# Second feed-forward layer of the last four groups as three products of high and low parts

## The chip, the cores and the metric

The kernel runs on one core of a Trainium2 chip. The core has TensorE (PE in the profile, its weight loads PEld), VectorE (DVE), ScalarE (ACT), GpSimd (POOL) and SyncE (SP), which run side by side and wait for each other through semaphores. The metric is the device time of one execution in microseconds (us); lower is better.

## The reference, cut to what matters

A graph layer is followed by a gated feed-forward layer. The change touches only the second matrix product of the feed-forward layer, `h @ w2`:

```python
x = x + gnn(layernorm(x), adj, ...)
h2 = layernorm(x)
weights = h2 @ wr + br                       # one weight for each node
sel_idx = top_k(weights, k)[:kk]             # 511 of 1024 nodes, for each of 8 batches
h = gelu(sel @ w1 + b1)                      # 128 -> 512
y = (h @ w2 + b2) * w_sel                    # 512 -> 128
x = x + h2 + scatter(y at sel_idx)
```

All values are 32-bit floats.

## The kernel before, in words

`build` writes one program for each engine by hand, so the order of the work on an engine is the order of its code, and semaphores (names in `_ok`, `_ps`, `_in`) carry results from one engine to another. First come eight batches of the graph layer. Then comes the feed-forward stage, in `NG = 9` groups b = 0..8 of 512 columns each: seven groups hold the chosen rows of batches 0 to 6, the last two hold all 1024 rows of batch 7. Buffers alternate with p = b % 2.

One group passes these steps:

- `sel_to_features(b)` (TensorE, L1577): four transposes bring the rows into bank D0. `hi_of_sel` (ScalarE, L881) rounds them to the fp32r format (high part, `xTH`), and `lo_of_sel` (VectorE, L1250) writes the rest (low part, `xTL`).
- `up(b, p, j)`, j = 0..3 (TensorE, L1590): the first layer. Each is done by `three` (L1353): high weight times high input, high times low, low times high, three fp32r matmuls of 512 columns into one of the banks C0, C1, D1 in turn.
- `gelu(b, p, j)` (ScalarE, L885) turns the bank into `g[p][j]`, plain fp32, in SBUF, and frees the bank.
- `down(b, p, j)` (TensorE, L1600): the second layer, one plain fp32 matmul of 512 columns with `wf2[:, j]` for each j, summed in bank N0 or N1. The profile records it as two halves.
- `update(b, p)` (ScalarE, L893) adds the bias, `update_back` (TensorE, L1613) transposes back into M0 (one buffer), `updated_rows(b, p)` (VectorE, L1274) scales and adds the base rows, and `rows_home` (GpSimd, L583) scatters each 128 rows into the output with an indirect DMA. For the last two groups `last_rows` (L1264) and a plain DMA take its place.

TensorE's order in a group is up(b,3), down(b,0), up(b+1,0), down(b,1), update_back(b-1), up(b+1,1), down(b,2), up(b+1,2), down(b,3), sel_to_features(b+2). The wait that matters later: up(b+1,0) needs `lo_of_sel(b+1)`, whose rows were transposed at the end of the group before. VectorE also ranks the weights of the last batch in groups 2 to 4 (`rank`) and ends that with `kept_weights` (L1254, three small instructions).

`wc2` holds the convolution weights, 128 partitions x 2 x (N_TAP x 128) fp32r. No matmul reads it after the last batch's convolution.

Of the kernel before, what the change touches and what calls it, by code (L numbers as in the profile page):

```python
# [19 lines left out]
ALU = mybir.AluOpType  # L20
ACT = mybir.ActivationFunctionType

P = 128
B = 8
N = 1024
T = N // P
D = 128
HALF = 512
# [13 lines left out]
HT = HID // D  # L42
# [15 lines left out]
UV_FOR = {0: 2, 1: 3, NU // 2: 4}  # L58
N2_AT = (5, 6, 7, 8)
EARLY = {3: 0, 7: 1, 11: 2}  # L60


C_ID, C_TRI, C_MASK = 0, P, 2 * P
# [31 lines left out]
V_BIH, V_BHH, V_F1, V_F2, V_BR, V_BSE, V_MSG = 8, 11, 14, 18, 19, 20, 21  # L95
# [51 lines left out]
def build(nc, x, adj, vectors, weights, conv2_w, const, out):  # L147
    ctx = ExitStack()
    with ctx:
        def sb(name, shape, dt=F32):  # L150
            return ctx.enter_context(nc.sbuf_tensor(name, shape, dt))
# [4 lines left out]
        def sem(name):  # L156
            return ctx.enter_context(nc.semaphore(name))

        def f32(ap):
            return ap.bitcast(F32)  # L160
# [10 lines left out]
        def col(k, n=1):  # L171
            return vec[:, k:k + n]
# [9 lines left out]
        wc2 = sb("wc2", [P, 2, N_TAP * D], F32R)  # L182

        def weight(at):
# [27 lines left out]
        wf2 = msgF[:, 0:HT, :]  # L212
# [14 lines left out]
        g = [[xflat[:, j * HALF:(j + 1) * HALF] for j in range(HT)],  # L227
             [xflat[:, (HT + j) * HALF:(HT + j + 1) * HALF] for j in range(2)] + [xT[:, 0, half_] for half_ in
                                                                                  (slice(0, HALF), slice(HALF, N))]]
# [31 lines left out]
        Db, Mb, Nb, Cb = (D0, D1), (M0, M1), (N0, N1), (C0, C1)  # L261
# [24 lines left out]
        c2_ps, xcH_ok, xcL_ok = sem("c2_ps"), sem("xcH_ok"), sem("xcL_ok")  # L286
# [18 lines left out]
        f1_ps, g_ok, f2_in = sem("f1_ps"), sem("g_ok"), sem("f2_in")  # L305
# [2 lines left out]
        y_ps, y_ok, yb_ps, O_ok = sem("y_ps"), sem("y_ok"), sem("yb_ps"), sem("O_ok")  # L308
        out_done = [sem("out_done0"), sem("out_done1")]
        place_ok, kept_ok, last_out = sem("place_ok"), sem("kept_ok"), sem("last_out")  # L310

        up_banks = (C0, C1, D1)
        LU = len(up_banks)

        def wait(eng, s, b, per, k):

            v = b * per + k
            if not isinstance(v, int) or v > 0:
                eng.wait_ge(s, v)
# [23 lines left out]
        def half(h):  # L343
            return slice(h * HALF, (h + 1) * HALF)
# [322 lines left out]
        def _(act):  # L667
# [70 lines left out]
            def row_of_weights(b, h, bank_):  # L738

                wait(act, wt_ps, b, NH, h + 1)  # L740
                wait(act, rank_ok, b - 1, T, T)
                nc.scalar.activation(W[:, half(h)], bank_[:, :], ACT.Copy).then_inc(W_ok, 1)  # L742
# [142 lines left out]
            def gelu(b, p, j):  # L885

                wait(act, f1_ps, b, HT, j + 1)
                if j == 0:
                    wait(act, y_ps, b - 2, 1, 1)
                nc.scalar.activation(g[p][j], up_banks[(HT * b + j) % LU][:, :], ACT.Gelu_apprx_tanh,  # L890
                                     bias=col(V_F1 + j)).then_inc(g_ok, 1)

            def update(b, p):  # L893
                wait(act, y_ps, b, 1, 1)
                wait(act, yb_ps, b - 2, 1, 1)
                nc.scalar.activation(Y[:, p, :], Nb[p][:, :], ACT.Identity, bias=col(V_F2)).then_inc(y_ok, 1)

            def ffn_step(b, q, first, last):
                if first:
                    hi_of_sel(0, 0)  # L900
                gelu(b, q, 0)
                if first:
                    candidate(B - 1, 1)
                    hi_of_sel(1, 1)
                gelu(b, q, 1)
                gelu(b, q, 2)
                if not first and not last:
                    hi_of_sel(b + 1, 1 - q)
                if b == 2:
                    row_of_weights(B - 1, 0, M1)  # L910
                if not first:
                    update(b - 1, 1 - q)
                gelu(b, q, 3)
                if b == 2:
                    row_of_weights(B - 1, 1, M1)

            over_groups(ffn_step)
            update(NG - 1, (NG - 1) % 2)
# [3 lines left out]
        def _(dve):  # L922
            TS, TT, STT = nc.vector.tensor_scalar, nc.vector.tensor_tensor, nc.vector.scalar_tensor_tensor
# [185 lines left out]
            def node_weights(b, q):  # L1109

                wait(dve, prod_ok, b, NH, NH)
                nc.vector.tensor_reduce(wv[:, :].rearrange("p (k t) -> p k t", k=NH), prod, mybir.AxisListType.X,
                                        ALU.add).then_inc(dot_ok, 1)
                wait(dve, dot_ok, b, 1, 1)
                TS(R[:, q, :, R_W], wv[:, :], col(V_BR), None, ALU.add).then_inc(w_ok, 1)
# [20 lines left out]
            def rank(b, q, t):  # L1136
                rank_tiles_ahead(b, q, t)
                rank_tiles_behind(b, q, t)
# [111 lines left out]
            def lo_of_sel(b, p):  # L1250
                wait(dve, xsH_ok, b, 1, 1)
                TT(xTL[:, 0, half(p)], D0[:, :], f32(xTH[:, 0, half(p)]), ALU.subtract).then_inc(xsL_ok, 1)

            def kept_weights():  # L1254

                b = B - 1
                dve.wait_ge(rank_ok, T * B)
                TT(acc[:, 1, :], acc[:, 1, :], acc[:, 2, :], ALU.add).then_inc(sum_ok, 1)
                dve.wait_ge(sum_ok, NH * b + 1)
                TT(rankF[:, :], acc[:, 0, :], acc[:, 1, :], ALU.add).then_inc(place_ok, 1)  # L1260
                dve.wait_ge(place_ok, 1)
                STT(kept[:, :], rankF[:, :], float(KEEP), R[:, 1, :, R_W], ALU.is_lt, ALU.mult).then_inc(kept_ok, 1)
# [11 lines left out]
            def updated_rows(b, p):  # L1274

                if b >= NXS:
                    last_rows(b, b - NXS)
                    return
                wait(dve, yb_ps, b, 1, 1)
                if b > 1:  # L1280
                    dve.wait_ge(out_done[p], 16 * TH * (b // 2))
                for c in range(TH):
                    xs = Xs[:, b, c, :]
                    STT(O[:, p, c, :], M0[:, c * P:(c + 1) * P], xs[:, R_W:R_W + 1], xs[:, D:2 * D], ALU.mult,  # L1284
                        ALU.add).then_inc(O_ok, 1)
# [27 lines left out]
            def ffn_step(b, q, first, last):  # L1313
                if first:
                    new_gate(B - 1, 1)
                    lo_of_sel(0, 0)
                    rank(B - 2, 0, 6)
                    rank(B - 2, 0, 7)
                    indices(B - 2, 0, 1)
                    blend(B - 1, 1)  # L1320
                    lo_of_sel(1, 1)
                    state_to_nodes(B - 1, (M1, N1))
                    moments2(B - 1)
                    mean_and_variance(1, stats2, T * B)
                elif not last:
                    lo_of_sel(b + 1, 1 - q)
                if b == 1:
                    last_norm()
                    last_products()
                    node_weights(B - 1, 1)  # L1330
                if b in (2, 3, 4):
                    rank(B - 1, 1, 3 * (b - 2))
                if not first:
                    updated_rows(b - 1, 1 - q)
                if b == 1:
                    last_base(0)
                    last_base(1)
                if b in (2, 3, 4):
                    rank(B - 1, 1, 3 * (b - 2) + 1)
                if b in (2, 3):  # L1340
                    rank(B - 1, 1, 3 * (b - 2) + 2)
                if b == 4:
                    kept_weights()

            over_groups(ffn_step)
# [4 lines left out]
        def _(pe):  # L1350
            MM, TR = nc.tensor.matmul, nc.tensor.transpose

            def three(out_, wgt, hi, lo, start, stop):  # L1353

                MM(out_, wgt(0), hi, start=start, stop=False)  # L1355
                MM(out_, wgt(0), lo, start=False, stop=False)  # L1356
                return MM(out_, wgt(1), hi, start=False, stop=stop)  # L1357
# [68 lines left out]
            def conv_odd(b):  # L1426
# [4 lines left out]
                for out_, at, row in ((N1[:, 0:Q], T_WOC, 0), (C0[:, 0:Q], T_WO, 1), (C0[:, Q:2 * Q], T_WO + KQ, 2)):  # L1431
# [4 lines left out]
                    for k in range(KQ):  # L1436
                        if n in EARLY:
                            front(b, EARLY[n])
                        n += 1
# [160 lines left out]
            def down(b, p, j):  # L1600
                wait(pe, g_ok, b, HT, j + 1)
                if j == 0:
                    if b == 0:
                        pe.wait_ge(f2_in, 16)
                        pe.wait_ge(q2_ok, NH * B)
                    if b == 1:
                        pe.wait_ge(x1_ok, NH * B)
                    wait(pe, y_ok, b - 2, 1, 1)
                i = MM(Nb[p][:, :], wf2[:, j, :], g[p][j], start=j == 0, stop=j == HT - 1)  # L1609
                if j == HT - 1:  # L1610
                    i.then_inc(y_ps, 1)

# [60 lines left out]
```

## Time and profile before

| | us |
|---|---|
| median of 3 runs | 564.97 (563.96 to 565.4) |
| the profiled execution, device time | 564.87 |
| its span, first to last instruction | 562.3 |
| TensorE busy | 545.6 (97%) |
| VectorE busy | 475.0 (84%) |
| ScalarE busy | 354.9 (63%) |
| GpSimd busy | 275.7 (49%) |

The device time lies 2.6 us above the span. Busy shares are means over the whole program, and matmuls are recorded longer than the step from one to the next, so the order of events in the stage decides, not the share. In the chain of waits (the work that ended last, followed back) each piece is the time that a step really added. Of the 40 slices of the page, the feed-forward stage is the last five or so (from about 488 us on); there TensorE shows 9 tenths throughout, while VectorE falls from 9 to 2 tenths after 530 us. The granted TensorE clock is 1.00 from 494 us to 555 us.

### The profile page before, as it was taken

How to read it: one execution, taken by the hardware profiler on the slowest of the kernel's cores; microseconds unless marked ns; L12 is line 12 of the kernel's file. 1: busy time of each engine (PE TensorE's matmuls, PEld its weight loads, DVE VectorE, ACT ScalarE, POOL GpSimd, SP SyncE). 2: the span in 40 equal slices, each digit the busy share in tenths (PEclk: the TensorE clock that was granted, in tenths of full speed). 3: DMA queues.
4: the chain of work that ended last, by engine and by line, in shares of the span. 5: the costliest groups of instructions: out<-in, count | busy, mean ns of one | idle time of the engine just before them, and what ended most of it. 6: DMA issues, size and time to landing. Idle time of an engine off the chain costs nothing.

```text
span 562.3 us, 9026 instructions
## 1 busy us (share of the span) xinstructions
PE 545.6 (97%) x2964; PEld 416.6 (74%) x2964; DVE 475.0 (84%) x1048; ACT 354.9 (63%) x616; POOL 275.7 (49%) x346
## 2 busy tenths in 40 slices
PE   7799999999999999999999999999999999899996
PEld 3786798678966896689767986798678966666663
DVE  6987478679898989899898989899979987978722
ACT  4856475856686577747674857575856673555552
POOL 2740354325358344834484546654545365536552
PEclk9999999999999999999999999999999999899999
DMA  8602700180008300650047001800171006402111
GB/s 274 278 2 76 300 0 2 45 308 23 2 0 270 142 2 1 193 220 1 1 124 289 1 2 52 323 2 1 46 283 46 1 1 191 148 16 81 36 36 61
DMA packets 33339, 54.52 MB, mean 97 GB/s; under 512 B 2098, under 2 KB 23051, under 8 KB 33166
## 3 DMA queue, kind: packets, MB, share of 16 engines
q1 hardware_dynamic: 29710, 48.42, 24.7%
q0 software_dynamic: 3584, 5.54, 2.8%
q8 instruction: 23, 0.38, 0.3%
q14 instruction: 22, 0.18, 0.1%
HBM read 44.21 MB, written 13.43 MB: 103 GB/s over the span
## 4 chain that ended last, share of the span: by engine, by line
PE 86%; DVE 8%; ACT 3%; DMA 2%; issue 1%; SPq 0%; DVEq 0%; ACTq 0%
PE N L1504 20%; PE M L1481 10%; PE C L1355 7%; PE C L1357 7%; PE C L1356 7%; PE D L1475 5%; PE N L1609 5%; PE N L1355 4%; PE N L1356 3%; PE N L1357 3%; ACT hab L674 2%; DVE tr L1014 2%; PE M L1356 2%; PE M L1355 2%; PE M L1357 2%; PE D L1355 2%
## 5 line engine op out<-in xcount | busy, mean ns | idle before, releaser
L780 ACT ACTIVATE tr<-D 128x512 f32<-128x512 f32 x128 | 76.4, 597 | 76.9 <-PE D L1475 75.2
L1481 PEld LDWEIGHTS M<-cst,adjb 128*128 128x128 f32 x512 | 63.9, 141 | 35.2 <-issue 21.2
L1475 PE MATMUL D<-V,U 128*128 128x512 f32 x128 | 89.3, 698 | 0.0
L1481 PE MATMUL M<-cst,adjb 128*128 128x128 f32 x512 | 76.8, 273 | 0.6 <-DVE ga L1101 0.6
L578 POOL DMA_INDIRECT sel<-R,ridx x56 | 61.1, 1090 | 16.0 <-issue 14.0
L1504 PE MATMUL N<-ga,msgF 128*128 128x512 f32 x128 | 64.2, 594 | 0.0
L1504 PE MATMUL N<-tz,msgF 128*128 128x512 f32 x128 | 64.2, 594 | 0.0
L1355 PE MATMUL C<-zR,wc 128*128 128x256 f32 x208 | 60.6, 291 | 0.6 <-DVE zR L1023 0.6
L1356 PE MATMUL C<-zR,wc 128*128 128x256 f32 x208 | 58.7, 282 | 0.0
L1357 PE MATMUL C<-zR,wc 128*128 128x256 f32 x208 | 58.6, 282 | 0.0
L1131 DVE TENSOR_SCALAR_CACHE_REDUCE junk<-W,R 128x1024 bf16<-128x1024 f32 (+3 forms) x64 | 51.7, 808 | 3.9 <-ACT W L742 3.9
L1101 DVE TENSOR_TENSOR ga<-tr,M 128x512 f32<-128x512 f32 x64 | 43.5, 680 | 9.6 <-ACT tr L780 9.4
L1101 DVE TENSOR_TENSOR tz<-tr,M 128x512 f32<-128x512 f32 x64 | 43.7, 684 | 8.5 <-ACT tr L780 6.7
L523 POOL TENSOR_TENSOR ga<-xT,gn 128x512 f32<-128x512 f32 x16 | 22.7, 1421 | 45.2 <-ACT gn L828 44.3
L624 POOL TENSOR_TENSOR wk<-tz,xT 128x512 f32<-128x512 f32 x8 | 12.4, 1556 | 61.2 <-DVE tz L1036 61.2
L1125 DVE TENSOR_SCALAR_CACHE_REDUCE junk<-W,R 128x128 bf16<-128x128 f32 (+6 forms) x56 | 41.4, 739 | 0.0
L1475 PEld LDWEIGHTS D<-V,U 128*128 128x128 f32 x128 | 24.3, 190 | 22.9 <-ACT tr L780 19.1
L605 POOL TENSOR_TENSOR junk<-hab 128x521 f32<-128x521 f32 x16 | 20.1, 1256 | 41.6 <-ACT hab L674 41.6
L1355 PEld LDWEIGHTS C<-zR,wc 128*128 128x128 f32 x208 | 39.3, 189 | 0.8 <-issue 0.8
L1356 PEld LDWEIGHTS C<-zR,wc 128*128 128x128 f32 x208 | 39.4, 189 | 0.0
L1357 PEld LDWEIGHTS C<-zR,wc 128*128 128x128 f32 x208 | 39.4, 189 | 0.0
L589 POOL DMA_INDIRECT out<-xn,adjb x28 | 28.4, 1013 | 20.3 <-DVE xn L1284 13.9
(236 smaller groups left out, 1527.6 us busy)
## 6 DMA issues: line engine op xcount, KB each, us to landing
adjb<-in_adj SPq DMA_DIRECT2D x8, 4096.0 KB, 14.9
adjb<-sel SPq DMA_DIRECT2D x7, 516.0 KB, 5.3
xall<-in_x SPq DMA_DIRECT2D x7, 512.0 KB, 5.2
out<-R SPq DMA_DIRECT2D x7, 512.0 KB, 3.5
R<-in_conv_w SPq DMA_DIRECT2D x1, 1088.0 KB, 8.6
sel<-R,ridx POOLq DMA_INDIRECT x56
xall<-in_weights SPq DMA_DIRECT2D x1, 832.0 KB, 11.0
xall<-in_x SPq DMA_DIRECT2D x2, 256.0 KB, 2.9
```

Of the source, the lines that this page charges most:

```text
L578: nc.gpsimd.indirect_dma_start(sel[b], bass.IndirectOffsetOnAxis(ap=ridx[:, q, t:t + 1], axis=0), R[:, q, t, :], None, bounds_check=KEEP - ...
L589: nc.gpsimd.indirect_dma_start(out_rows, bass.IndirectOffsetOnAxis(ap=at, axis=0), O[:, p, c, :], None, bounds_check=B * N - 1, oob_is_err ...
L780: nc.scalar.activation(E[:, u % NE, :], Db[u % NH][:, :], ACT.Exp, scale=-1.0).then_inc(exp_ok, 1)
L1101: TT(A[u % NA], E[:, u % NE, :], Mb[u % NH][:, :], ALU.mult).then_inc(A_ok, 1)
L1125: TS(junk[:, t % 2, 0:t * P], W[:, 0:t * P], R[:, q, t, R_W:R_W + 1], None, ALU.is_ge, ALU.add, accum_out=acc[:, 0, t:t + 1])
L1131: TS(junk[:, k, t * P:N], W[:, t * P:], w, None, ALU.is_gt, ALU.add, accum_out=acc[:, 1, t:t + 1])
L1355: MM(out_, wgt(0), hi, start=start, stop=False)
L1356: MM(out_, wgt(0), lo, start=False, stop=False)
L1357: return MM(out_, wgt(1), hi, start=False, stop=stop)
L1475: MM(Db[h][:, :], U[:, t * P:(t + 1) * P], V[:, half(h)], start=True, stop=True).then_inc(d_ps, 1)
L1481: i = TR(Mb[h][:, k * P:(k + 1) * P], adjb[:, h * TH + k, t * P:(t + 1) * P], ident)
L1504: MM(Nb[h][:, :], msgF[:, t, :], A[v % NA], start=t == 0, stop=t == T - 1).then_inc(nm_ps, 1)
```

## The change

Groups 5 to 8 (`b >= G3`, `G3 = 5`) compute `down` with `three` as well. That needs high and low parts of the weights and of the activations; both lie in `wc2`. ScalarE writes the high part of `wf2` (`hi_of_f2`, in group 3) and VectorE its low part (`lo_of_f2`, in group 4). Of the activations, ScalarE writes the high part for j = 0 and j = 3, by a second evaluation of the gelu from the same bank ahead of the plain one; VectorE copies it for j = 1 and j = 2 and subtracts for all four (`parts_of_g`). `kept_weights` moves from VectorE's group 4 to group 5.

```diff
+G3 = 5
+        f2S = wc2[:, :, 0:HT * D]
+        def g_parts(p, j):
+            at = HT * D + (HT * p + j) * HALF
+            return wc2[:, :, at:at + HALF]
 # ScalarE, gelu
-                nc.scalar.activation(g[p][j], up_banks[(HT * b + j) % LU][:, :], ACT.Gelu_apprx_tanh,
+                up_ = up_banks[(HT * b + j) % LU]
+                if b >= G3 and j in (0, HT - 1):
+                    nc.scalar.activation(g_parts(p, j)[:, 0], up_[:, :], ACT.Gelu_apprx_tanh, bias=col(V_F1 + j))
+                nc.scalar.activation(g[p][j], up_[:, :], ACT.Gelu_apprx_tanh,
                                      bias=col(V_F1 + j)).then_inc(g_ok, 1)
+            def hi_of_f2():
+                act.wait_ge(f2_in, 16)
+                act.wait_ge(c2_ps, 2 * B)
+                nc.scalar.activation(f2S[:, 0], wf2[:, :, :].rearrange("p j d -> p (j d)"),
+                                     ACT.Copy).then_inc(f2H_ok, 1)
 # ScalarE, end of a group
+                if b == G3 - 2:
+                    hi_of_f2()
 # VectorE
+            def lo_of_f2():
+                dve.wait_ge(f2H_ok, 1)
+                TT(f2S[:, 1], wf2[:, :, :].rearrange("p j d -> p (j d)"), f32(f2S[:, 0]),
+                   ALU.subtract).then_inc(f2L_ok, 1)
+            def parts_of_g(b, p, j):
+                wait(dve, g_ok, b, HT, j + 1)
+                gp = g_parts(p, j)
+                if j not in (0, HT - 1):
+                    nc.vector.tensor_copy(gp[:, 0], g[p][j]).then_inc(gH_ok, 1)
+                    dve.wait_ge(gH_ok, 2 * (b - G3) + j)
+                TT(gp[:, 1], g[p][j], f32(gp[:, 0]), ALU.subtract).then_inc(gL_ok, 1)
 # VectorE, a group, after lo_of_sel(b + 1)
+                if b == G3 - 1:
+                    lo_of_f2()
...
+                if b == G3:
+                    parts_of_g(b, q, 1)
+                    parts_of_g(b, q, 2)
+                if b >= G3:
+                    parts_of_g(b, q, HT - 1)
+                    if not last:
+                        parts_of_g(b + 1, 1 - q, 0)
                 if not first:
                     updated_rows(b - 1, 1 - q)
+                if b >= G3 and not last:
+                    parts_of_g(b + 1, 1 - q, 1)
+                    parts_of_g(b + 1, 1 - q, 2)
+                if b == G3 - 1:
+                    parts_of_g(b + 1, 1 - q, 0)
...
-                if b == 4:
+                if b == G3:
                     kept_weights()
 # TensorE, down
-                i = MM(Nb[p][:, :], wf2[:, j, :], g[p][j], start=j == 0, stop=j == HT - 1)
+                if b < G3:
+                    i = MM(Nb[p][:, :], wf2[:, j, :], g[p][j], start=j == 0, stop=j == HT - 1)
+                else:
+                    if b == G3 and j == 0:
+                        pe.wait_ge(f2L_ok, 1)
+                    wait(pe, gL_ok, b - G3, HT, j + 1)
+                    gp = g_parts(p, j)
+                    i = three(Nb[p][:, :], lambda v: f2S[:, v, j * D:(j + 1) * D], gp[:, 0], gp[:, 1],
+                              j == 0, j == HT - 1)
```

TensorE at the start of group 5, before the change: the transposes of group 6's rows into D, then up(5,3), down(5,0), up(6,0), down(5,1) and the transposes back into M.

```order
L1587 MATMUL D<-cst,adjb 128x128 [waits xsL_ok,sel_in6]
L1587 MATMUL D<-cst,adjb 128x128 x3
L1355 MATMUL D<-xTH,wall 128x512 [waits g_ok,xsL_ok]
L1356 MATMUL D<-xTL,wall 128x512
L1357 MATMUL D<-xTH,wall 128x512
L1609 MATMUL N<-xall,msgF 128x512 [waits y_ok,g_ok]
L1355 MATMUL C<-xTH,wall 128x512 [waits g_ok,xsL_ok]
L1356 MATMUL C<-xTL,wall 128x512
L1357 MATMUL C<-xTH,wall 128x512
L1609 MATMUL N<-xall,msgF 128x512 [waits g_ok]
L1619 MATMUL M<-cst,wk 128x128 [waits y_ok,O_ok]
```

The same place after the change (L1404 to L1406 are `three`).

```order
L1636 MATMUL D<-cst,adjb 128x128 [waits xsL_ok,sel_in6]
L1636 MATMUL D<-cst,adjb 128x128 x3
L1404 MATMUL D<-xTH,wall 128x512 [waits g_ok,xsL_ok]
L1405 MATMUL D<-xTL,wall 128x512
L1406 MATMUL D<-xTH,wall 128x512
L1404 MATMUL N<-wc 128x512 [waits f2L_ok,gL_ok,y_ok,g_ok]
L1405 MATMUL N<-wc 128x512
L1406 MATMUL N<-wc 128x512
L1404 MATMUL C<-xTH,wall 128x512 [waits g_ok,xsL_ok]
L1405 MATMUL C<-xTL,wall 128x512
L1406 MATMUL C<-xTH,wall 128x512
L1404 MATMUL N<-wc 128x512 [waits gL_ok,g_ok]
```

Nothing changes its place on TensorE; each down into N becomes three matmuls from `wc2`, and the first of them waits for `gL_ok` besides.

VectorE from the end of group 4 to group 6, before: `kept_weights` (three rows), `lo_of_sel(6)`, `updated_rows(4)`, `lo_of_sel(7)`.

```order
L1258 TENSOR_TENSOR acc<-acc 128x8 [waits rank_ok]
L1260 TENSOR_TENSOR rankF<-acc 128x8 [waits sum_ok]
L1262 SCALAR_TENSOR_TENSOR kept<-rankF,R 128x8 [waits place_ok]
L1252 TENSOR_TENSOR xTL<-D,xTH 128x512 [waits xsH_ok]
L1284 SCALAR_TENSOR_TENSOR xn<-M,adjb 128x128 [waits out_done0,yb_ps]
L1284 SCALAR_TENSOR_TENSOR xn<-M,adjb 128x128 x3
L1252 TENSOR_TENSOR xTL<-D,xTH 128x512 [waits xsH_ok]
```

After, from `updated_rows(4)` (L1319) to `lo_of_sel(7)` (L1272). Ahead of this piece, between `lo_of_sel(6)` and `updated_rows(4)`, stand CAST and TENSOR_TENSOR for g(5,1), the same for g(5,2), and one TENSOR_TENSOR each for g(5,3) and g(6,0).

```order
L1319 SCALAR_TENSOR_TENSOR xn<-M,adjb 128x128 [waits out_done0,yb_ps]
L1319 SCALAR_TENSOR_TENSOR xn<-M,adjb 128x128 x3
L1285 CAST wc<-xall 128x512 [waits g_ok]
L1287 TENSOR_TENSOR wc<-xall,wc 128x512 [waits gH_ok]
L1285 CAST wc<-xall 128x512 [waits g_ok]
L1287 TENSOR_TENSOR wc<-xall,wc 128x512 [waits gH_ok]
L1293 TENSOR_TENSOR acc<-acc 128x8 [waits rank_ok]
L1295 TENSOR_TENSOR rankF<-acc 128x8 [waits sum_ok]
L1297 SCALAR_TENSOR_TENSOR kept<-rankF,R 128x8 [waits place_ok]
L1272 TENSOR_TENSOR xTL<-D,xTH 128x512 [waits xsH_ok]
```

`lo_of_sel(7)` followed `updated_rows(4)` directly before; now seven instructions stand between them, four of them of 512 columns.

## Rows read from the trace of the kernel before

**Rows 1.** The page, part 1: busy us, share of the span, instructions.

```profile
PE 545.6 (97%) x2964; PEld 416.6 (74%) x2964; DVE 475.0 (84%) x1048; ACT 354.9 (63%) x616; POOL 275.7 (49%) x346
```

**Rows 2.** Windows: stretch, length, busy of each engine, clock, DMA share, GB/s.

```profile
541.00:548.00 7.00, 7.00 (x28) 4.33 (x27) 1.81 (x5) 3.59 (x7) 3.88 (x4) 1.00 0.11 37
```

**Rows 3.** Chain of waits, from 480 us on: start us, us added, engine, tile, line.

```profile
530.53 0.44 PE D L1587 x4
...
533.34 0.86 PE N L1609 x2
...
537.75 0.44 PE D L1587 x4
538.19 0.23 PE C L1355
...
539.75 0.35 PE C L1355
...
540.56 0.86 PE N L1609 x2
...
544.97 0.43 PE D L1587 x4
...
552.88 1.72 PE N L1609 x4
...
555.03 1.73 PE N L1609 x4
```

**Rows 4.** Timeline, ScalarE, 538 us: start us, us, engine, line, operation.

```profile
538.23 0.60 ACT L883 ACTIVATE xTH<-D 128x512 fp32r<-128x512 f32 x1 [0.61 <-PE D L1587]
538.72 0.68 ACT L896 ACTIVATE wk<-N,vec 128x512 f32<-128x512 f32 x1
539.29 0.69 ACT L890 ACTIVATE xall<-C,vec 128x512 f32<-128x512 f32 x1
```

**Rows 5.** Timeline, VectorE, 530 to 539 us.

```profile
530.22 0.17 DVE L1258 TENSOR_TENSOR acc<-acc 128x8 f32<-128x8 f32 x1
...
530.62 0.17 DVE L1262 SCALAR_TENSOR_TENSOR kept<-rankF,R 128x8 f32<-128x8 f32 x1
531.63 0.69 DVE L1252 TENSOR_TENSOR xTL<-D,xTH 128x512 fp32r<-128x512 f32 x1 [0.84 <-ACT xTH L883]
534.68 1.13 DVE L1284 SCALAR_TENSOR_TENSOR xn<-M,adjb 128x128 f32<-128x128 f32 x4 [2.35 <-PE M L1619]
538.86 0.69 DVE L1252 TENSOR_TENSOR xTL<-D,xTH 128x512 fp32r<-128x512 f32 x1 [3.06 <-ACT xTH L883]
```

**Rows 6.** Groups of VectorE by form: busy us, mean ns, idle before.

```profile
L1005 DVE TENSOR_TENSOR xTL<-xT,xTH 128x512 fp32r<-128x512 f32 x16 | 10.4, 684 | 0.5 <-ACT xTH L805 0.5
...
L1131 DVE TENSOR_SCALAR_CACHE_REDUCE junk<-W,R 128x512 bf16<-128x512 f32 x8 | 5.9, 741 | 0.0
...
L998 DVE MEMSET hab<- 128x1044 f32 x1 | 0.9, 928 | 0.2 <-issue 0.2
```

**Rows 7.** Timeline, GpSimd beside VectorE, 401 to 414 us.

```profile
401.83 2.18 POOL L568 TENSOR_TENSOR R<-xall,R 128x1024 f32<-128x1024 f32 x1
...
403.27 0.89 DVE L1132 SCALAR_TENSOR_TENSOR junk<-W,R,cst 128x128 bf16<-128x128 f32 x1
...
406.67 1.09 DVE L1088 SCALAR_TENSOR_TENSOR zR<-wk,zR 128x512 fp32r<-128x512 f32 x1
...
406.86 1.74 POOL L578 DMA_INDIRECT sel<-R,ridx  x1 [0.30 <-issue]
...
412.74 0.97 POOL L578 DMA_INDIRECT sel<-R,ridx  x1 [0.30 <-issue]
...
412.89 0.35 DVE L1132 SCALAR_TENSOR_TENSOR junk<-W,R,cst 128x128 bf16<-128x128 f32 x1
```

**Rows 8.** Timeline, GpSimd, its last scatter.

```profile
554.15 0.97 POOL L589 DMA_INDIRECT out<-xn,adjb  x1 [0.30 <-issue]
```

**Rows 9.** DMA issues: KB each, median us from issue to landing.

```profile
out<-xn,adjb POOLq DMA_INDIRECT x28, 2.3
```

More of the change, by code:

```diff
@@ L310, in build @@
         place_ok, kept_ok, last_out = sem("place_ok"), sem("kept_ok"), sem("last_out")
+        gL_ok, f2H_ok, f2L_ok, gH_ok = sem("gL_ok"), sem("f2H_ok"), sem("f2L_ok"), sem("gH_ok")
+        f2S = wc2[:, :, 0:HT * D]
+        def g_parts(p, j):
+            at = HT * D + (HT * p + j) * HALF
+            return wc2[:, :, at:at + HALF]
         up_banks = (C0, C1, D1)
```

## The prediction

> **What bounds the kernel now.** I read the page's busy shares first: TensorE is busy 545.6 of the 562.3 us [rows 1]. Then the windows over the tail, since the change lives there: in the seven microseconds from 541 us TensorE is busy for all 7.00, ScalarE 3.59, VectorE 1.81, GpSimd 3.88, at a granted clock of 1.00 [rows 2]. So TensorE's stream is the bound in groups 5 to 8, and VectorE and ScalarE have room on average. Third, the chain of waits, because it gives what each step really adds: a plain fp32 down is 0.86 us, each fp32r matmul of `three` 0.23 us, four transposes 0.44 us [rows 3]. From one `sel_to_features` to the next is 544.97 - 537.75 = 7.22 us, a group.
>
> The chain also has a small wait in each group: the first matmul of up(b+1,0) is 0.35 us instead of 0.23 at 539.75 [rows 3]. The timelines say why. The transposes end at 538.19; `hi_of_sel` runs 538.23 to 538.83, `lo_of_sel` 538.86 to 539.55 [rows 4, 5]; the next down starts at 540.56 [rows 3]. Less three matmuls (0.69) the first one begins at 539.87, so a low part that ends at time t lets TensorE begin at t + 0.32. This chain is independent of how long down(b,0) takes. It is the row that limits what the change can give.
>
> **The sum, part by part.** All of it is made against the profiled execution (564.87 us, 2.6 above its span); that lies 0.1 under the median 564.97.
>
> Removed and added on TensorE: 16 downs (groups 5 to 8, j = 0..3). Each goes from 0.86 to 3 x 0.23 = 0.69 or 0.70; I take a saving of 0.165. 16 x 0.165 = 2.65 us, if nothing else waits.
>
> Taken back by `lo_of_sel`: in groups 5, 6, 7 up(b+1,0) already waits 0.12 us for it, so the saving of down(b,0) turns into a longer wait. 3 x 0.165 = 0.5 us. That leaves 2.15 us as the most the order of the code can give.
>
> ScalarE: `hi_of_f2` once (0.62 us or so) falls into group 3, where ScalarE is half idle. The second gelus are two per group. Consecutive ScalarE instructions start 0.57 us apart (538.72 to 539.29 [rows 4]), so ScalarE goes from 3.6 to 4.7 us in a group of about 6.6: hidden. up(b+1,3) needs the bank of gelu(b+1,0), which is free three microseconds earlier. Cost zero.
>
> VectorE: what it did in a group was `lo_of_sel` and `updated_rows`, 1.81 us. Now come four subtractions and two copies. A 512-column subtraction of two SBUF tensors takes 0.684 us [rows 6]; when nothing makes it wait for the one ahead, the next starts 0.60 after its start. An instruction that waits for the one ahead starts 0.03 after its end (530.22 + 0.17 to 530.42 for the three of `kept_weights`, which take 0.57 from start to end [rows 5]).
>
> The copy (CAST, fp32 to fp32r, SBUF to SBUF, one input) is not in the trace. Bounds by the nearest rows: above, a one-input VectorE instruction of 512 columns, 0.741 us; below, the memset of 1044 columns in 0.928 us, half of which is 0.46 [rows 6]. Below that I know no row, and a longer one than 0.74 only if something holds it (below). I take 0.46, since the memset is the other instruction here that only moves data, and keep 0.74.
>
> The Trainium skill, "VectorE: DVE Perf Modes", section on the perf-mode tier table, says that a copy of fp32 within SBUF runs at two elements a cycle and a two-tensor operation at one. Worked out from its formula, an estimate, the copy would take 0.42 us, and the sum would be about 0.2 us better. The trace's 0.684 for the subtraction agrees with one element a cycle; its one-input row at 0.741 (a reduce) does not show the fast form.
>
> Now the order. Group 5 begins as before: transposes of group 6's rows end at 530.97, `lo_of_sel(6)` runs 531.63 to 532.32 [rows 3, 5]. VectorE then copies g(5,1), 532.23 to 532.69, and subtracts to 533.41. down(5,1) can begin at 533.73; before it began at 533.34 [rows 3]. That is 0.39 late, in spite of the saving of down(5,0). The three downs that follow save 0.49, so the transposes of group 7's rows end at about 538.09 (before 538.19).
>
> On VectorE after 533.3: second copy and subtraction (1.09), subtractions for g(5,3) and g(6,0) (1.2), `updated_rows(4)` 535.6 to 536.7 (before 534.68 [rows 5]), then copy, subtraction, copy, subtraction (2.2), then `kept_weights` (0.5). `lo_of_sel(7)` can start at 539.35, where its input is ready at 538.09 + 0.67 = 538.76. It is 0.6 late. It ends at 540.04, up(7,0) runs 540.36 to 541.05, where it had ended at 540.56: now 0.49 behind. Three downs give 0.49 back: at the end of group 6 the change has gained nothing so far.
>
> Group 6: VectorE has no `kept_weights`, but waits for gelu(7,0) (done about 542.35) before it may take `updated_rows(5)` at 543.0; copies and subtractions end so that `lo_of_sel(8)` starts at 546.2, 0.1 late. up(8,0) ends at 547.88 against 547.78. Group 7: three downs, -0.49, net -0.39. Group 8 has no up to wait for: four downs, -0.66, net -1.05. Its tightest wait is g(8,3): up(8,3) ends about 552.5, two gelus and a subtraction end at 554.5, TensorE may start at 554.83 and gets there at 555.03. It just fits.
>
> What stands behind the moved steps: `updated_rows(b-1)` now follows a subtraction that waits for gelu(b+1,0), so it comes 0.4 to 1 us later, and so do the four scatters on GpSimd's queue behind it. The last of these ended at 555.12 and lands 2.3 us after issue [rows 8, 9], before the final rows of a program that ends past 561. Four us of room; cost zero. M0, which `updated_rows` frees, is wanted again five microseconds later.
>
> Sum: 564.87 - 2.65 + 0.5 (the old wait) + 1.1 (VectorE late: 0.39 for down(5,1), 0.6 for `lo_of_sel(7)`, 0.1 for `lo_of_sel(8)`) = 563.82. Against the median, 563.9.
>
> **The rivals.**
>
> A. VectorE is in time. If the copies or the small steps are shorter than I take them, or GpSimd and VectorE overlap better, only the 0.5 us is lost: 564.97 - 2.15 = 562.8. For it: VectorE's 1.81 us in 7 [rows 2]. Against it: the queue ahead of `lo_of_sel(7)` is 7 us of work in a window of 6.4, whatever the copy takes down to about 0.3.
>
> B. Slower: GpSimd holds the copies. VectorE and GpSimd get in each other's way in this trace: a two-input VectorE instruction of 128 columns took 0.89 us while a GpSimd tensor operation ran, against 0.35 elsewhere; an indirect DMA that began inside a two-input VectorE instruction took 1.74 us against 0.97 [rows 7]. But the same two-input instruction ran in its 0.35 beside an indirect DMA in flight (412.74 and 412.89 [rows 7]). What a fast copy does beside one, no row shows. Six copies stand ahead of something that TensorE waits for (four between `lo_of_sel(6)` and `lo_of_sel(7)`, two more ahead of `lo_of_sel(8)`), and the scatters of `rows_home` run for 5.1 of each 7 us. If each copy is held 0.5 us on average, half an indirect DMA, 6 x 0.5 = 3.0: 563.9 + 3.0 = 566.9. It decides from 0.2 us a copy (6 x 0.175 = 1.05 eats the gain); fully held, 0.97 each, it would be 569.7.
>
> The Trainium skill, "SBUF — State Buffer", section on the two separate sides, says just this: a fast-form copy and a GpSimd operation share a port pair under an exclusive lock, the first keeps it for its whole length, and descriptors of indirect DMAs are held up. By that rule the copies make GpSimd late, which costs nothing here, and may be held themselves. The row of 1.74 us agrees with the first half; no row here shows the second.
>
> C. The copy has no fast form and takes as long as the subtraction or the one-input row, 0.69 to 0.74. Six copies, 0.23 to 0.28 longer each: +1.4 to +1.7, so 565.3 to 565.6, no change that can be seen. For it: the slow one-input row. Against it: the memset.
>
> **Chances.** A change under 0.3%, 1.7 us, can't be told from none here; the three runs of before spread over 1.4 us. Forecast 0.50, A 0.15, B 0.15, C 0.20. Faster by over 1.7 us: nearly all of A and a quarter of the forecast, 0.27. Slower by over 1.7 us: most of B, 0.13. The rest, 0.60, is within. The forecast's own range is 563.2 to 564.6. The given range must take in A (562.8) and C (565.6) and part of B: 562.4 to 566.2.
>
> **What would show it.** Right: in the chain of waits the downs of groups 5 to 8 as three pieces of 0.23; groups 5 and 6, from one `sel_to_features` to the next, near 7.1 and 7.3 us and not near 6.7; TensorE waiting for VectorE (`gL_ok`) at down(5,1) and for `lo_of_sel` at up(7,0) by about 0.8 us; the CAST near 0.46 us. A shows as no such wait at up(7,0); B as CASTs of widely different lengths, or as VectorE idle ahead of them while GpSimd runs, and C as a CAST of 0.69. I am wrong altogether if a matmul from `wc2` takes more than 0.23, if down(8,3) waits long for g(8,3), or if the time moves outside this tail.

## The result, and the profile after

The changed kernel takes 565.78 us (median of 16 runs, 565.21 to 566.59) against 564.58 (16 runs, 563.96 to 565.88): a ratio of 1.0021, 95% interval 1.0015 to 1.0028, so 1.2 us slower. I had forecast 563.9, 1.1 us faster than the 564.97 of three runs then known, in the range 562.4 to 566.2. The time is inside the range and on the wrong side.

The profiled execution took 566.05 us with a span of 563.9, 1.6 longer than the span before. The page, part 1, as [rows 1], and the windows view, as [rows 2]:

```profile
PE 543.9 (96%) x2980; PEld 419.3 (74%) x2980; DVE 489.3 (87%) x1073; ACT 360.1 (64%) x625; POOL 277.3 (49%) x346
```

```profile
541.00:548.00 7.00, 6.81 (x33) 5.32 (x33) 5.16 (x11) 4.59 (x9) 3.84 (x5) 1.00 0.11 36
```

TensorE has lost 1.7 us of work and is no longer busy throughout; VectorE went from 1.81 to 5.16 us in these seven. The chain of waits (start us, us added, what) follows the path that the prediction drew, as [rows 3] did:

```profile
530.90 0.45 PE D L1636 x4
531.35 0.02 issue
531.38 0.61 ACT xTH L891
531.99 0.02 issue
532.01 0.69 DVE xTL L1272
532.70 0.53 DVE wc L1285
...
547.05 0.61 DVE xTL L1272
547.66 0.04 issue
547.70 0.50 PE D L1404
...
555.77 0.24 PE N L1404
556.01 0.23 PE N L1405
556.24 0.25 PE N L1406
```

From 532 to 547 it lies mostly on VectorE (between 540.8 and 543.7, left out here, on TensorE and ScalarE), and the downs are three pieces of 0.23 to 0.25, as forecast. Now the ends. The last down ended at 555.03 + 1.73 = 556.76 [rows 3]; it ends at 556.49 here, although this execution was 0.37 late on entering the stretch (530.90 against 530.53). So TensorE gained 0.64 us from there on. VectorE's last rows, in its timeline:

```profile
558.01 1.13 DVE L1307 SCALAR_TENSOR_TENSOR R<-M,kept,R 128x128 f32<-128x128 f32 x4 [1.68 <-PE M L1676]
```

They end at 559.14 (559.41 before). Every row that the chain shows is earlier at the end, and yet the span is 1.6 longer. What is later is on GpSimd, which the chain does not touch. The timeline of VectorE from 547 us (compare the `updated_rows` at 549.12 in the kernel before, not in the rows above) and that of GpSimd, as [rows 8]:

```profile
548.52 0.69 DVE L1287 TENSOR_TENSOR wc<-xT,wc 128x512 fp32r<-128x512 f32 x1 [0.87 <-ACT xT L901]
550.01 0.69 DVE L1287 TENSOR_TENSOR wc<-xall,wc 128x512 fp32r<-128x512 f32 x1 [0.80 <-ACT xall L901]
550.62 1.12 DVE L1319 SCALAR_TENSOR_TENSOR xn<-M,adjb 128x128 f32<-128x128 f32 x4
```

```profile
551.81 1.10 POOL L597 DMA_INDIRECT out<-xn,adjb  x1 [1.76 <-DVE xn L1319]
553.22 0.97 POOL L597 DMA_INDIRECT out<-xn,adjb  x1 [0.30 <-issue]
554.50 0.97 POOL L597 DMA_INDIRECT out<-xn,adjb  x1 [0.31 <-issue]
555.77 0.97 POOL L597 DMA_INDIRECT out<-xn,adjb  x1 [0.30 <-issue]
```

VectorE waits for gelu(8,0), subtracts its high part at 550.01, and only then makes `updated_rows(6)`. The last scatter starts at 555.77 instead of 554.15 and ends at 556.75 instead of 555.12, 1.63 later. Behind it the records hold one more instruction that the views do not count as busy, GpSimd's closing DRAIN (its own records, us from the span's start; SyncE's last one beside it):

```
         GpSimd's last work ends   its DRAIN ends   SyncE's DRAIN   span
before            555.12               562.06          561.98       562.3
after             556.75               563.69          561.70       563.9
```

The DRAIN ends 6.94 us after GpSimd's last work in both. (Its record begins while the scatters still run, at 551.75 in the kernel before, so only its end says anything here.) Before, it tied with SyncE, which had waited for the last rows to land; after, SyncE is 0.28 earlier and GpSimd 1.63 later, and the span follows GpSimd. Of both, 0.37 is this execution's late entry into the stretch: without it SyncE is 0.65 earlier and GpSimd 1.26 later, and that is the 1.2 us of the medians. The waits of SyncE's queue (waited for: us in total, times, longest) show it under another engine's name, first the kernel before, then the changed one:

```profile
SPq L149 <- PEq L149: 0.3, 1, 0.3
```

```profile
SPq L150 <- PEq L150: 2.2, 1, 2.2
```

### The profile page after: what moved, and what is told of

The parts are those of the page before. It is cut to its first block, busy times and chain, and to the rows that moved or that the text cites. A ratio compares the mean times of both kernels' runs of the same rounds, so it can differ in the third digit from the quotient of the medians.

```text
span 563.9 us, 9106 instructions
## 1 busy us (share of the span) xinstructions
PE 543.9 (96%) x2980; PEld 419.3 (74%) x2980; DVE 489.3 (87%) x1073; ACT 360.1 (64%) x625; POOL 277.3 (49%) x346
## 4 chain that ended last, share of the span: by engine, by line
PE 82%; DVE 12%; ACT 3%; issue 1%; DMA 1%; POOL 0%; DVEq 0%; ACTq 0%; POOLq 0%
PE N L1553 20%; PE M L1530 10%; PE C L1404 7%; PE C L1405 7%; PE C L1406 7%; PE D L1524 5%; PE N L1404 4%; PE N L1405 3%; PE N L1406 3%; PE N L1659 2%; ACT hab L682 2%; DVE tr L1034 2%; PE M L1405 2%; PE M L1404 2%; PE M L1406 2%; PE D L1404 2%
## 5 line engine op out<-in xcount | busy, mean ns | idle before, releaser
L1404 PE MATMUL C<-zR,wc 128*128 128x256 f32 x208 | 60.5, 291 | 0.6 <-DVE zR L1043 0.6
L1406 PE MATMUL C<-zR,wc 128*128 128x256 f32 x208 | 58.5, 281 | 0.0
L1404 PEld LDWEIGHTS C<-zR,wc 128*128 128x128 f32 x208 | 39.2, 189 | 0.8 <-issue 0.8
L597 POOL DMA_INDIRECT out<-xn,adjb x28 | 29.7, 1062 | 20.2 <-DVE xn L1319 13.8
L1406 PEld LDWEIGHTS C<-zR,wc 128*128 128x128 f32 x208 | 39.3, 189 | 0.0
```

Source lines behind the costliest of these rows:

```text
L597: nc.gpsimd.indirect_dma_start(out_rows, bass.IndirectOffsetOnAxis(ap=at, axis=0), O[:, p, c, :], None, bounds_check=B * N - 1, oob_is_err ...
```

## The experiments

Theory G: the program ends when both SyncE's path and GpSimd's last work + 6.94 us have ended, and the change made the second late. The rivals: the 1.2 us sit on the path itself, in VectorE's added work and the stalls that it gives TensorE (V in the expectations); or TensorE, whose code is longer, comes late to the end of the program (T; its own closing DRAIN says no, it ends at 558.02 after 558.30 before); or they come from the scatters as transfers, in how long they take and land, and not from GpSimd's end as such. Times below are medians; ratios are to the kernel before in the same session, with 95% intervals. Executions enter group 5 at slightly different times; the transposes ahead of it start at 530.36 us in the profile of the kernel before and at 530.74 in that of the changed one, and where another profile's start matters it is given.

**e1: `updated_rows` ahead of the subtraction of g(b+1,0).**

```diff
                 if b >= G3:
                     parts_of_g(b, q, HT - 1)
-                    if not last:
-                        parts_of_g(b + 1, 1 - q, 0)
                 if not first:
                     updated_rows(b - 1, 1 - q)
                 if b >= G3 and not last:
+                    parts_of_g(b + 1, 1 - q, 0)
```

> The changed kernel with updated_rows(b-1) put ahead of the subtraction for g(b+1,0) on VectorE in groups 5 to 7; same instructions. Three theories of the 1.2 us that the change cost. G: the program ends with GpSimd's closing DRAIN, 6.94 us after the end of its last scatter (555.12 to 562.06 before, 556.75 to 563.69 after), and the scatter is late because updated_rows(6) starts at 550.62 instead of 549.12. V: VectorE's late low parts cost TensorE, as in rival C of the prediction. T: TensorE comes late to the closing barrier because its code is longer. G expects updated_rows(6) some 0.8 us earlier and the time 0.7 to 1.1 us below the changed kernel's, with the drain still last. V expects at most 0.3 us, from group 6. T expects no change.

Measured: 565.48 us, 1.0015 (1.0006 to 1.0024). GpSimd's timeline:

```profile
550.75 1.37 POOL L597 DMA_INDIRECT out<-xn,adjb  x1 [0.85 <-DVE xn L1319]
552.42 1.21 POOL L597 DMA_INDIRECT out<-xn,adjb  x1 [0.30 <-issue]
553.93 0.97 POOL L597 DMA_INDIRECT out<-xn,adjb  x1 [0.30 <-issue]
555.21 0.97 POOL L597 DMA_INDIRECT out<-xn,adjb  x1 [0.30 <-issue]
```

The rows came 1.08 earlier (549.54), but the first two scatters took 1.37 and 1.21 us, because they now started inside a VectorE subtraction or copy (all such cases are counted in the last section). 0.57 of it reached the last scatter's end (556.18), and the span fell by 0.6 (0.14 of both is an earlier start of the stretch). The profile moves as G says, but the time fell by only 0.3 us; G had expected 0.7 to 1.1 and V at most 0.3, so this run does not decide between them.

**e2: in the kernel before, two spare additions ahead of `updated_rows(6)`.**

```diff
+                if b == NXS:
+                    TT(tz[:, 0, :], tr[:, 0, :], tr[:, 1, :], ALU.add)
+                    TT(tz[:, 1, :], tr[:, 0, :], tr[:, 1, :], ALU.add)
                 if not first:
                     updated_rows(b - 1, 1 - q)
```

> The kernel before, with two more 512-column additions (into a tile that nobody reads any more) on VectorE just ahead of updated_rows(6): 1.2 us of VectorE work at a place where TensorE waits for nothing from VectorE. G expects the last scatter 1.2 us minus VectorE's idle time there later; the idle time is 2.36 us and ends when the transposes are there, so the additions must run before them and the delay may be as small as 0. If it is 0, then this run says nothing on G. V and T expect no change.

Measured: 564.30 us, 0.9999 (0.9990 to 1.0008). The additions ran in the time in which VectorE waited for the transposes anyway; the last scatter ended at 555.13, where it had been. My experiment delayed nothing, so it says nothing; e8 repeats it properly.

**e3: the changed kernel without its last scatter.** It leaves 128 output rows of batch 6 unwritten (SyncE's wait for their landing is lowered to match).

```diff
-                for c in range(TH):
+                for c in range(TH - (b == NXS - 1)):
```

> The changed kernel without the very last scatter of group 6 (the output rows of 128 chosen nodes of batch 6 are left out); GpSimd's last scatter then ends 1.27 us earlier. G expects the time 1.2 to 1.3 us below the changed kernel's, which is at or a little below the kernel before. V and T expect no change.

Measured: 564.24 us, 0.9996 (0.9987 to 1.0005), by the ratios 1.4 us below the changed kernel. VectorE and TensorE do all that they did; GpSimd's last rows are these:

```profile
552.62 0.97 POOL L597 DMA_INDIRECT out<-xn,adjb  x1 [0.30 <-issue]
553.89 0.97 POOL L597 DMA_INDIRECT out<-xn,adjb  x1 [0.30 <-issue]
```

Last work ends 554.86, DRAIN 561.72, SyncE 561.09, span 562.0. (The stretch starts 0.58 earlier here, so of the 1.97 by which the DRAIN moved 1.39 are the edit's.) The whole loss hangs on the end of GpSimd's queue. VectorE's work and TensorE's stalls are all still there, so the loss wasn't in them. That the scatters as transfers are late could still claim it.

**e4: the kernel before, with a tiny GpSimd memset that waits for the rows of group 7.**

```diff
+            pool.wait_ge(O_ok, TH * (NXS + 1))
+            nc.gpsimd.memset(psum[:, :], 0.0)
```

> The kernel before, with one tiny memset on GpSimd after its last scatter, which waits for the rows of group 7 (written at 556.2), so that GpSimd's last work ends about 1.1 us later than now while its last scatter stays where it is. Two forms of G: if the 6.9 us of the closing DRAIN belong to the scatters (their queue must empty), the time stays; if they follow any last GpSimd work, the time rises by about 1.2 us. V and T expect no change.

```profile
554.35 0.97 POOL L589 DMA_INDIRECT out<-xn,adjb  x1 [0.30 <-issue]
556.46 0.10 POOL L665 MEMSET psum<- 128x8 f32 x1 [1.14 <-DVE R L1274]
```

Measured: 565.40 us, 1.0017 (1.0008 to 1.0026). The last scatter moved by 0.20 (554.15 to 554.35), nothing waits for the memset, and the program is 1.0 us slower: the DRAIN ends at 563.50, again 6.94 after the last work, and the span is 563.7. SyncE's DRAIN ends at 562.43, 0.45 later than before (0.20 of it from a later start of the stretch, 530.56), which alone would give a span of 562.7. So it is not the scatters' transfer or landing but the end of whatever GpSimd does last.

**e8: e2 with a wait for the transposes ahead of the additions, so that they must delay `updated_rows(6)`.**

```diff
                if b == NXS:
+                    wait(dve, yb_ps, b - 1, 1, 1)
                     TT(tz[:, 0, :], tr[:, 0, :], tr[:, 1, :], ALU.add)
```

> The kernel before, with two additions of 512 columns on VectorE between the arrival of group 6's transposes and updated_rows(6). TensorE waits for nothing that this delays (M0 is next written 4 us later). G expects GpSimd's last scatter and the time 1.2 us later, 565.6. V and T expect no change.

```profile
550.27 1.12 DVE L1284 SCALAR_TENSOR_TENSOR xn<-M,adjb 128x128 f32<-128x128 f32 x4
```

Measured: 565.83 us, 1.0023 (1.0014 to 1.0032). This is the kernel before in all of TensorE's work, with only `updated_rows(6)` moved from 549.12 to 550.27. Its last scatter ends at 556.28, its DRAIN at 563.22, SyncE's at 561.94 as before. It reproduces the change's loss by that one delay.

**e6, e7, e5: which part of the change makes the rows late.** e6 lets ScalarE write every high part, so VectorE's copies and their waits in groups 5 to 8 (two a group, eight in all) go:

```diff
-                if b >= G3 and j in (0, HT - 1):
+                if b >= G3:
...
-                if j not in (0, HT - 1):
-                    nc.vector.tensor_copy(gp[:, 0], g[p][j]).then_inc(gH_ok, 1)
-                    dve.wait_ge(gH_ok, 2 * (b - G3) + j)
```

> The changed kernel with ScalarE writing the high part of all four g tiles; VectorE loses its eight copies (3.9 us of work with their gaps), ScalarE gains eight gelus of 0.57 us. V expects lo_of_sel(7) on time, TensorE's last matmul 1.0 to 1.5 us earlier than in the changed kernel. G expects updated_rows(6) and so the end 1.0 to 1.5 us earlier: 564.3 to 564.8. A third view, that ScalarE becomes the bound (five to six us of work in a group of 6.6), expects no gain.

e7 puts `kept_weights` back into group 4:

```diff
-                if b == G3:
+                if b == 4:
                     kept_weights()
```

> The changed kernel with kept_weights (three small VectorE instructions, 0.56 us) back in group 4. V expects lo_of_sel(7) and all that follows 0.5 us earlier, and with G the time 0.5 us below the changed kernel's, 565.3. If VectorE's lateness is made up again later, the time stays.

e5 is e1, e6 and e7 together:

> The changed kernel with three edits: ScalarE writes the high part of all four g tiles (no copy on VectorE), kept_weights goes back to group 4, and updated_rows(b-1) stands ahead of the subtraction for g(b+1,0). If GpSimd's last work plus 6.94 us ends the program (theory G) and VectorE's queue ahead of lo_of_sel sets TensorE's pace in groups 5 to 7 (theory V, the part of the prediction on that), then lo_of_sel(7) and (8) start as soon as their input is there, groups 5 and 6 take about 6.7 us each, updated_rows(6) starts near 547.8 and the time is 1.0 to 1.6 us below the kernel before (562.9 to 563.5). If V were wrong, TensorE would be no earlier than in the changed kernel and the time about that of the kernel before.

Measured, with the ends as above:

```
     time     ratio (95%)                last work  DRAIN    SyncE    span
e6   564.62   1.0004 (0.9995 to 1.0013)   555.73    562.67   561.05   562.9
e7   565.29   1.0016 (1.0007 to 1.0025)   556.08    563.02   561.01   563.3
e5   564.01   0.9991 (0.9982 to 1.0000)   554.92    561.86   560.38   562.1
```

Against the changed kernel the DRAIN ends 1.0 us earlier without the copies, 0.7 without the move of `kept_weights` and 0.6 with the other order (e1). Some 0.15 of each is the start of the stretch (530.57, 530.56 and 530.60 against 530.74), which leaves 0.85, 0.5 and 0.4; by the ratios it is 1.0, 0.3 and 0.3, each known to about 0.6 us. In e5 the last down ends at 555.16, 1.3 us before the changed kernel's and 1.6 before the kernel before, with a start (530.35) like the latter's; SyncE's path gained 1.6. The span gained 0.2, since the DRAIN gained only 0.2. TensorE's saving is real and is not paid out.

**e9, e10, e11: bring the last scatter forward.** In groups 5 to 7 the transposes back go into the gap in which TensorE waits for `lo_of_sel`, and `updated_rows` goes ahead of the subtraction of g(b,3). e9 adds both to e5, e11 adds both to the changed kernel, e10 puts only the transposes forward in the kernel before.

```diff
-                    if j == 1 and not first:
+                    if j == (0 if b in (5, 6, 7) else 1) and not first:
                         update_back(b - 1, 1 - q)
```

```diff
-                if b >= G3:
+                if last:
                     parts_of_g(b, q, HT - 1)
                 if not first:
                     updated_rows(b - 1, 1 - q)
                 if b >= G3 and not last:
+                    parts_of_g(b, q, HT - 1)
```

> The combined kernel (ScalarE writes all highs, kept_weights in group 4, rows early) with one more move: in groups 5, 6 and 7 TensorE makes update_back(b-1) right after down(b,0), in the gap in which it waits for lo_of_sel anyway, and VectorE makes updated_rows(b-1) right after lo_of_sel(b+1), ahead of the subtraction of g(b,3). By the theory that GpSimd's last work + 6.94 us ends the program: updated_rows(6) moves from 548.25 to about 546.5, the last scatter ends near 553.3 instead of 554.92, the closing DRAIN near 560.2 instead of 561.86, and then SyncE's own path (560.38, itself 0.2 earlier or later) is as late: time 562.3 to 562.9, 1.5 to 2.1 us below the kernel before. By the theory that TensorE's or VectorE's end decides (557.8 for VectorE's last row, moved by 0.2 at most): 563.8 to 564.2, no change from the combined kernel.

> The kernel before with only that early update_back in groups 5 to 7, none of the change. TensorE gives up 0.36 us of transposes later and makes them in its gap; from the rows (gap to 546.81, y_ok at 546.62) I work out 0.15 saved per group, 0.45 in all at the last down. GpSimd's last work ends near 553.2 instead of 555.12, the DRAIN near 560.1 instead of 562.06, so that SyncE's path (561.98 before, about 561.5 here) decides alone. The theory: 0.4 to 0.5 us faster, 563.9 to 564.1. If only GpSimd's end counted, 1.9 faster (562.6); if the transposes in the gap hold up(b+1,0) by as much as they save, 564.4.

> The changed kernel with the two moves only (early update_back in groups 5 to 7, updated_rows right after lo_of_sel), VectorE's copies and kept_weights as the change has them. updated_rows(6) moves from 550.62 to about 547.9, the last scatter's end from 556.75 to about 554.2, the DRAIN from 563.69 to about 561.2; SyncE's path from 561.7 to about 561.3. The theory that GpSimd's last work + 6.94 us decides: 2.2 to 2.5 us below the changed kernel, 563.4 to 563.7. If the change's loss sat in VectorE's copies or in TensorE's stalls, which stay, 565.3 to 565.8.

```
     time     ratio (95%)                last work  DRAIN    SyncE    span
e9   563.75   0.9974 (0.9963 to 0.9985)   554.68    561.63   560.15   561.9
e10  564.54   0.9992 (0.9982 to 1.0001)   554.02    560.96   562.43   562.7
e11  564.86   0.9997 (0.9986 to 1.0009)   555.50    562.45   561.95   562.7
```

e11 takes the changed kernel back to the time of the kernel before, 0.24% of it (1.4 us) by the ratios and 1.2 by the spans, with nothing of the copies removed. I had expected 2.2 or more. The rows of group 6 came at 548.92 and not at 547.9, and the last scatters were stretched besides, one of them to 1.43 us:

```profile
546.71 0.60 ACT L891 ACTIVATE xTH<-D 128x512 fp32r<-128x512 f32 x1 [1.51 <-PE D L1636]
```

```profile
551.40 1.43 POOL L597 DMA_INDIRECT out<-xn,adjb  x1 [0.30 <-issue]
```

The first row is where the 1.0 us of the rows began: the transposes that `hi_of_sel(8)` waits for are recorded to end at 545.60, and it starts 1.11 us after that instead of the usual 0.04. `update(6)` stands behind it on ScalarE, the transposes back behind that (548.03), and `updated_rows(6)` last.

e10 shows the other side. GpSimd's end came 1.1 us earlier and bought nothing by itself, as SyncE's path is then the later one. That profile entered group 5 already 0.83 us late (its transposes at 531.19 against 530.36 in the kernel before, ahead of any edited step; more on this below); from there SyncE's path gained 0.38, near the 0.45 that I had worked out. The median is 0.5 below, its interval just reaches no change, so the gain is likely and not shown.

e9 is the fastest here, 0.26% below the kernel before (0.15 to 0.37%) and the only one whose interval lies clear of it. It stayed short of its expectation, 1.5 to 2.1 below, for two reasons. `updated_rows(6)` came at 547.50, not 546.5: its semaphore from TensorE arrived at 547.48, though the transposes are recorded to end at 546.60. And all four last scatters were stretched by subtractions in which they started:

```profile
548.71 1.37 POOL L597 DMA_INDIRECT out<-xn,adjb  x1 [2.30 <-DVE xn L1316]
550.38 1.19 POOL L597 DMA_INDIRECT out<-xn,adjb  x1 [0.30 <-issue]
551.87 1.08 POOL L597 DMA_INDIRECT out<-xn,adjb  x1 [0.30 <-issue]
553.26 1.43 POOL L597 DMA_INDIRECT out<-xn,adjb  x1 [0.31 <-issue]
```

Such late signals of TensorE's transposes stand in e9, e10 and e11 alone, the three kernels with the moved transposes, and in all three one stands in group 3, ahead of every step that was moved. VectorE starts `updated_rows(2)` 0.45 to 0.51 us after the recorded end of its transposes, where the other ten profiles have 0.04. The kernel before, and e10:

```profile
520.17 1.12 DVE L1284 SCALAR_TENSOR_TENSOR xn<-M,adjb 128x128 f32<-128x128 f32 x4 [0.75 <-PE M L1619]
```

```profile
521.00 1.13 DVE L1284 SCALAR_TENSOR_TENSOR xn<-M,adjb 128x128 f32<-128x128 f32 x4 [1.23 <-PE M L1619]
525.99 0.50 PE L1355 MATMUL D<-xTH,wall 128*128 128x512 f32 x1 [0.40 <-issue]
```

That made VectorE's ranking and `lo_of_sel(5)` late, TensorE sat idle for 0.34 to 0.40 us ahead of up(5,0) (the second row of e10), and all three entered group 5 0.4 to 0.5 us later than they would have. It is a part of what e9 and e11 fell short by. What in the edit brings it on stays open.

In e9 the DRAIN is still 1.5 us later than SyncE, so more lies there. The size of its gain is less sure than the interval says: its session had a slower kernel before (565.01 us, and 564.42 to 564.58 in the others), and the profile of the kernel before, 0.4 us above e9's in span, is of an earlier session.

In all 13 profiles the span ends 0.2 to 0.3 us after the later of the DRAIN and SyncE's end.

## Why the prediction was wrong

- **Right in kind: TensorE's sum.** I forecast a net 1.05 us on TensorE; it was 0.64, and groups 5 and 6 took 7.38 and 7.39 us (from one `hi_of_sel` to the next: 531.38, 538.76, 546.15) instead of 7.1 and 7.3. The three-matmul downs cost 0.69 to 0.70, the wait of down(5,1) came (0.42 us idle at 534.14), and so did that of up(7,0) for `lo_of_sel(7)` (0.69). What was mis-sized is VectorE's lateness, 1.1 forecast and 1.5 measured: counted from group 5's start, `lo_of_sel(7)` began at 540.07 - 0.37 = 539.70 (forecast 539.35) and `lo_of_sel(8)` at 546.60 (546.2).
- **The copy.** I took 0.46, bounds 0.46 and 0.74. Six of the eight took 0.41 to 0.45; the two that started 0.62 and 0.65 us into a scatter took longer:

```profile
532.62 0.60 DVE L1285 CAST wc<-xall 128x512 fp32r<-128x512 f32 x1
...
533.92 0.58 DVE L1285 CAST wc<-xT 128x512 fp32r<-128x512 f32 x1
...
537.38 0.42 DVE L1285 CAST wc<-xall 128x512 fp32r<-128x512 f32 x1
```

  Rival C (0.69 and more) is out, though the measured 565.78 lies just above its 565.3 to 565.6. That the time fell inside the stated range is luck: the upper part stood there for B and C, and it was neither. (The prediction held that a change under 0.3% can't be told from none; with 16 runs of each kernel this one of 0.21% can.) This trace agrees with the two elements a cycle that the Trainium skill states for this copy ("VectorE: DVE Perf Modes", the perf-mode tier table; an estimate of 0.42 us).
- **Rival B** put the loss on the same pair of engines but on the wrong one. Two of eight copies were held, by 0.15 us, not each by 0.5. The scatters were held: the first behind `updated_rows(6)` took 1.10 us instead of 0.97, and in e11 one took 2.30. Subtractions do it as well as copies: e9 has no copies, and scatters that started inside its subtractions took up to 1.94 us. The row of 1.74 us [rows 7], which the prediction took as agreeing with a rule on fast-form copies, stood beside a two-input instruction as well. The prediction had said that the copies "make GpSimd late, which costs nothing here".
- **The step that failed.** "Four us of room; cost zero", for the scatters behind the moved `updated_rows`. I forecast the rows 0.4 to 1 us late; `updated_rows(6)` was 1.50 late (549.12 to 550.62) and the last scatter's end 1.63, or 1.13 and 1.26 without the late entry of this execution. So the lateness was nearly as forecast, and its price was not. And there was no room: I measured it from the landing (2.3 us after issue [rows 9]) to the final rows past 561, where GpSimd's own end was 555.12 + 6.94 = 562.06, level with SyncE's 561.98. So any delay of GpSimd's last work was paid in full, as e8 and e4 show. Without the late entry, SyncE's path moved by -0.65 us, which is what the sum was about, and GpSimd's by +1.26, which is what came.
- **What a view could have told.** Little. The kernel before had 0.3 us at "SPq L149 <- PEq L149", and e10, where SyncE itself is last, has 0.2, so the 0.3 says at most that another engine was level with SyncE. The ends of the DRAINs say it outright. I looked at neither, and took the end of the chain of waits for the end of the program.

## What to carry to other kernels

Before you call a late step on a side engine free, find what closes the program on each engine: here GpSimd's closing DRAIN ends 6.9 us after its last work, be it a scatter or a tiny memset, and a saving on TensorE is paid out only as far as that path moves too. When a kernel scatters with GpSimd up to its tail, put the producers of the last scatter ahead of any work that only fills a gap (e8 shows the price of the contrary, e11 and e9 the way back). And an experiment that is to delay a step must be placed behind the wait that the step itself has; in front of it (e2) it fills idle time. Read the profile of an experiment from ahead of its edit: e9 to e11 lost time two groups before the first moved step.

## What the runs showed of the hardware

- GpSimd's closing DRAIN ended 6.94 us after the end of its last work in 12 of 13 profiles (6.86 in e3), after a scatter as after a memset of 0.10 us (e4). No view counts it as busy. What GpSimd does in that time no run shows.
- A copy from fp32 to fp32r of 128 x 512 within SBUF takes 0.41 to 0.45 us on VectorE; the two that started 0.62 to 0.65 us into a scatter of 0.97 took 0.58 to 0.60, in each of the five profiles that have copies. Those that started inside a scatter which was itself stretched took 0.42 to 0.45.
- A scatter on GpSimd is held when it starts inside one of the 512-column subtractions or copies of `parts_of_g`. From 530 us on, the 13 profiles have 45 such scatters; they took 1.01 to 2.30 us, but for one of 0.97. Of the 146 others all took 0.97 or 0.98 but three (1.08 twice beside VectorE's ranking, 1.27 beside e2's additions), though 53 of them had such an instruction start while they ran. In the changed kernel the mean over all 28 scatters rose from 1.01 to 1.06 us.
- VectorE or ScalarE, waiting for TensorE's transposes, starts 0.04 us after their recorded end; in e9, e10 and e11 it started 0.21 to 1.11 us after it in two or three places each. Why stays open.
